# Three shared-expert tiles moved from behind the first router's picks into the last iterations of attention

## What is computed

```python
x = x + cross_attention(layernorm(x), ctx)        # 8 heads of 32, 77 keys
x = x + ffn0(layernorm(x))    # 8 experts of 704, top 2 of 8 by softmax, and a shared expert of 352:
                              # (silu(h @ Sg) * (h @ Su)) @ Sd for every row
x = x + patches(layernorm(x)) # a matmul with W_in and a lookup by a running count
x = x + ffn1(layernorm(x))    # 32 experts of 128, top 6 in groups, and a shared expert of 512
```

## Time and profile before

| | |
|---|---|
| median of 3 runs | 775.14 us (771.28 to 779.2) |
| the profiled execution | 776.99 us, of which its span 775.2 us |
| PE busy | 689.3 us, 89% of the span |
| DVE, ACT, POOL busy | 54%, 36%, 40% |
| granted TensorE clock | 0.947 of full speed on average |

### The profile page before, as it was taken

One profiled execution on the slowest core, in us unless ns is written; L12 is line 12 of the kernel. 1 busy time (PEld: TensorE's weight loads), 2 busy tenths in 40 slices (PEclk: granted clock), 3 DMA queues, 4 the chain that ended last, 5 costly groups with the idle time before them and its releaser, 6 DMA issues.

```text
span 775.2 us, 14150 instructions
## 1 busy us (share of the span) xinstructions
PE 689.3 (89%) x4526; PEld 611.6 (79%) x4526; DVE 415.7 (54%) x1613; ACT 276.4 (36%) x620; POOL 308.1 (40%) x322
## 2 busy tenths in 40 slices
PE   3868888999999999999999989889786999989836
PEld 2657677899999999999999979866554999978724
DVE  3998947423333343444684367457521666667823
ACT  2545743222111111133222322242321677767510
POOL 2323410770001010100035504554774477777770
PEclk9897966999999999999999999999989899999988
DMA  8999998236767676855587853363667777788976
GB/s 260 396 323 263 259 248 233 104 109 241 249 210 235 211 236 211 287 191 178 180 299 249 296 181 133 133 227 120 217 208 216 257 237 249 229 328 285 364 252 247
DMA packets 93535, 181.23 MB, mean 234 GB/s; under 512 B 9857, under 2 KB 54998, under 8 KB 93182
## 3 DMA queue, kind: packets, MB, share of 16 engines
q1 hardware_dynamic: 78048, 138.67, 57.5%
q0 software_dynamic: 13344, 38.68, 13.2%
q10 hardware_dynamic: 2046, 2.71, 1.1%
HBM read 134.07 MB, written 65.62 MB: 258 GB/s over the span
## 4 chain that ended last, share of the span: by engine, by line
PE 65%; DVE 13%; POOL 7%; DMA 6%; issue 5%; ACT 2%; DVEq 1%; SPq 0%; POOLq 0%; ACTq 0%
PE PB L596 22%; PE PB L634 14%; PE PB L610 6%; POOL rows_out L1891 4%; PE PB L803 3%; PE PB L794 3%; POOL rows_in L1852 3%; DMA X<-in_x 2%; PE PB L782 2%; PE PB L740 2%; PE PB L661 2%; DMA MEM<-rows_out 2%; PE PB L578 1%; DVE WK L1231 1%; DVE M L1240 1%
## 5 line engine op out<-in xcount | busy, mean ns | idle before, releaser
L596 PE MATMUL PB<-XT,MEM 128*128 128x128 f32 x1584 | 185.0, 276 | 0.3 <-issue 0.3
L596 PEld LDWEIGHTS PB<-XT,MEM 128*128 128x128 f32 x1584 | 180.7, 192 | 0.6 <-issue 0.5
L1843 POOL DMA_INDIRECT sorted_y<-WK x36 | 34.5, 959 | 244.2 <-DVE WK L1445 243.3
L1852 POOL DMA_INDIRECT rows_in<-MEM x96 | 93.9, 979 | 45.4 <-issue 28.5
L634 PE MATMUL PB<-MEM,WK 128*128 x432 | 101.3, 385 | 1.9 <-DVE MEM L1606 1.9
L634 PEld LDWEIGHTS PB<-MEM,WK 128*128 128x128 f32 x432 | 80.7, 193 | 12.1 <-issue 2.3
L917 ACT ACTIVATE XT<-PB 128x256 f32<-128x256 f32 x52 | 19.8, 381 | 146.2 <-PE PB L578 146.2
L1891 POOL DMA_INDIRECT rows_out<-WS,MEM x58 | 57.0, 983 | 32.7 <-issue 15.6
L803 PE MATMUL PB<-MEM,WK 128*128 x228 | 59.8, 386 | 8.3 <-DVE WK L1784 8.0
L1891 POOL DMA_INDIRECT rows_out<-MEM x56 | 54.7, 977 | 17.1 <-issue 15.5
L926 ACT ACTIVATE WK<-PB 128x640 f32<-128x640 f32 x36 | 25.3, 703 | 83.8 <-PE PB L596 83.8
(11 more groups left out here) (279 smaller groups left out, 1232.9 us busy)
## 6 DMA issues: line engine op xcount, KB each, us to landing
MEM<-in_w SPq DMA_DIRECT2D x36, 896.0 KB, 7.1
rows_in<-in_consts SPq DMA_DIRECT2D x32, 600.0 KB, 12.2
MEM<-in_w SPq DMA_DIRECT2D x36, 512.0 KB, 3.7
MEM<-rows_in SPq DMA_DIRECT2D x58, 300.0 KB, 3.9
MEM<-rows_out SPq DMA_DIRECT2D x16, 768.0 KB, 7.7
MEM<-in_w SPq DMA_DIRECT2D x32, 256.0 KB, 3.5
MEM<-in_w SPq DMA_DIRECT2D x2, 3072.0 KB, 19.0
sorted_x<-MEM SPq DMA_DIRECT2D x1, 5070.0 KB, 40.5
```

Source lines behind the costliest of these rows:

```text
L596: t = e.matmul(o[:, to:to + P], UPW[m][i % (3 - m)][:, k, c * P:(c + 1) * P], XT[:, n % 2, k, :], start=(k == 0), stop=(k == 1))
L1843: e.indirect_dma_start(out=DY, out_offset=bass.IndirectOffsetOnAxis(ap=DEST[:, i:i + 1], axis=0), in_=YS[:, i % 2, :], in_offset=None).the ...
L1852: e.indirect_dma_start(out=DX1, out_offset=bass.IndirectOffsetOnAxis(ap=SLOT1[:, i, j:j + 1], axis=0), in_=XR[:, i, :], in_offset=None).th ...
```

## The change

`FILL = 3`: shared tiles 0, 1 and 2 are taken out of the item loop, which now starts at n = 3, and their parts are written into the last iterations by hand, for PE, ACT and DVE. `EARLY` stays 14; SP and POOL are unchanged.

- **PE.** turn_x(0) at the end of iteration 17, turn_x(1) at the end of 18. The gate half of tile 0 at the head of 18, its up half behind values(15). The gate half of tile 1 at the end of 19; in 20 its up half between router(11) and the turns of tiles 12 and 13, and down(0) behind these. Behind the loop turn_x(2), down(1), the gate half of tile 2, then the counting matmuls, which now also wait for h(0), then tile 2's up half and turn_x(3).
- **Banks.** Tile 0 uses banks 5 and 2, the turned inputs the upper half of bank 7 and then bank 5. So the first half waits until the last probabilities are copied out ("pt", 15).
- **ACT.** The copies of turned inputs 0 and 1 at the end of 17 and 18; gates(0) in 19 and gates(1) in 21, each behind `turned_rows` and ahead of `router_rows`; the copy for tile 2 in 22; gates(2) behind the exponential.
- **DVE.** hidden(0) behind the statistics of iteration 19. hidden(1) between `max` and `max_index` of the first part of the picks, result(0) behind that `max_index`, result(1) behind "mm". hidden(2) and then the expert table behind "slot0". The three instructions for the shares stand at the end of the chain to "slot0" instead of ahead of the wait for the counts.

```diff
-EARLY = 14
+EARLY, FILL = 14, 3
...
-            return (0, 2) if n >= EARLY + nb else (3 * (n % 2), 3 * (n % 2) + 1)
+            return (5, 2) if n == 0 else (0, 2) if n >= EARLY + nb else (3 * (n % 2), 3 * (n % 2) + 1)
+
+        def turn_place(n):
+            return PB[:, 7, D:2 * D] if n < 2 else PB[:, 5, 0:D] if n < FILL else PB[:, 6, 0:D]
...
+            def shared_up(n, m, nb=NBLK):
+                q.wait_ge("xtb", n)
+                q.wait_ge("in_ws")
+                if n < FILL:
+                    q.wait_ge("s1", NT - 1)
+                    q.wait_ge("pt", NT - 1)
...
             for n in range(NT + 7):
                 if 0 <= n - 1 < NT:
                     scores(n - 1)
                 if n < NT:
                     queries(n, routed)
+                if n == NT + 2:
+                    shared_up(0, 0)
                 for i in ROUTED.get(n, ()):
                     router(i, n)
                 if 0 <= n - 3 < NT:
                     values(n - 3)
                 if 0 <= n - 2 < NT:
                     turn_probs(n - 2)
+                if n == NT + 2:
+                    shared_up(0, 1)
+                if n == NT + 4:
+                    shared_up(1, 1)
                 for i in ROWS.get(n - 1, ()):
                     router_turn(i, n)
                     routed[i % 2] = i
+                if n in (NT + 1, NT + 2):
+                    turn_x(n - NT - 1, NBLK)
+                if n == NT + 3:
+                    shared_up(1, 0)
+                if n == NT + 4:
+                    down(0, NBLK)
...
-            q.wait_ge("lgc", 1)
-            turn_x(0, NBLK)
+            turn_x(2, NBLK)
+            down(1, NBLK)
+            shared_up(2, 0)
+            q.wait_ge("h", 0)
             q.wait_ge("mm")
...
+            shared_up(2, 1)
+            turn_x(FILL, NBLK)
-            for n in range(SPLIT):
+            for n in range(FILL, SPLIT):
...
+                if n in (NT + 3, NT + 5):
+                    gates((n - NT - 3) // 2, NBLK)
+                if n == NT + 6:
+                    turned_x(2)
...
+            gates(2, NBLK)
+            turned_x(FILL)
...
                     if n > NT:
                         finish()
+                        hidden(0, NBLK)
...
                     t = e.max(m8[:, i, :], LG0[:, i, :])
                 t.then_inc(*q.mark("l0_v"))
-                q.wait_ge(*q.last)
+                t = q.last
+                if k == 0:
+                    hidden(1, NBLK)
+                q.wait_ge(*t)
                 for i in range(lo, hi):
                     t = e.max_index(i8[:, i, :], m8[:, i, :], LG0[:, i, :])
                 t.then_inc(*q.mark("l0_v"))
+                if k == 0:
+                    result(0, NBLK)
...
+            placed = q.last
+            q.wait_ge("pre")
+            e.tensor_scalar(PR[:, 0, :], PR[:, 1, :], 1.0, None, ALU.add).then_inc(*q.mark("l0_v"))
...
-            for n in range(SPLIT):
+            hidden(2, NBLK)
+            expert_table()
+            for n in range(FILL, SPLIT):
```

More of the change, by code:

```diff
@@ L541, in router @@
                 t.then_inc(*q.mark("lg", i))
[L543 to L559, removed]
             regs, busy = {}, {}
@@ L601, in up @@
                 else:
-                    q.wait_ge("xtb", n)
-                    q.wait_ge("in_ws")
                     q.wait_ge("h", n - 1 if n >= EARLY + nb else n - 2)
[L605 to L612, removed]
+                    for m in range(2):
+                        shared_up(n, m, nb)
                     between(n, nb)
@@ L895, in patches @@
                              ACT.Copy).then_inc(*q.mark("dpa", k))
[L897 to L912, removed]
             def turned_x(n):
                 q.wait_ge("tx", n)
+                q.wait_ge("scores", NT - 1)
                 q.wait_ge("up1", n - 2)
-                e.activation(XT[:, n % 2, :, :].rearrange("p c t -> p (c t)"), PB[:, 6, 0:D], ACT.Copy).then_inc(
+                e.activation(XT[:, n % 2, :, :].rearrange("p c t -> p (c t)"), turn_place(n), ACT.Copy).then_inc(
                     *q.mark("xtb", n))
@@ L1265, in dve_program @@
             e.tensor_copy(TRB[:], CC[:, CTR:CTR + P]).then_inc(*q.mark("trb"))
[L1267 to L1289, removed]
-                q.wait_ge(*q.last)
-                for i in range(lo, hi):
-                    t = e.max_index(i8[:, i, :], m8[:, i, :], LG0[:, i, :])
-                t.then_inc(*q.mark("l0_v"))
@@ L1459, in block_iteration @@
                     hidden(n, nb)
+            for n in range(NT + 7):
+                if 0 <= n - 1 < NT:
+                    scores(n - 1, n % 4 == 3 and n + 1 < NT or n % 4 == 1 and n > 8 or n == 16)
+                if 0 <= n - 4 < NT:
+                    stats(n - 4, "st", "o2", n - 4)
+                if 0 <= n - 3 < NT:
+                    values(n - 3)
+                for f, *k in jobs.get(n, ()):
+                    f(*k)
+                if n % 4 == 3 and 4 <= n < NT + 4:
+                    behind.append(norm_steps(n // 4 - 1, ("st", n - 4), False))
+                    if n > NT:
+                        finish()
+                        hidden(0, NBLK)
+                if n == NT + 4:
+                    logits(0, 0, NT - 4)
@@ new lines, in dve_program, with tiles @@
+            result(1, NBLK)
+            PRE = PB[:, 5, 0:128].rearrange("p (t e) -> p t e", t=NT)
+            upto, before = PAGE_U[:, 8:40].rearrange("p (g e) -> p g e", g=4), PAGE_U[:, 0:32].rearrange(
+                "p (g e) -> p g e", g=4)
+            ge = T1.rearrange("p (g t e) -> p g t e", g=4, t=4)
+            def tiles(v):
+                return v.unsqueeze(2).broadcast_to([P, 4, 4, 8])
+            for v in (PAGE_U[:, 0:8], PAGE_G[:, 0:1], PAGE_F[:, 0, :]):
+                t = e.memset(v, 0.0)
```

219 lines of the change are left out of this document (131 added, 88 removed).

## The result

The changed kernel takes 779.82 us (median of 20 executions, 774.83 to 785.8), the kernel before 776.33 (20 executions on the same chip, 769.5 to 781.31). The ratio is 1.0059, 95% interval 1.0036 to 1.0081: slower by 0.6%, 4.6 us by the ratio and 3.5 by the medians. The forecast was +5.6 us.

The account below looks back on a forecast made before the run. Two chains, PE's tiles and the scatter's weights 4.15 us ahead, bound block 0's start; block 0 +4.6 us from a late "slot0", plus 1.0 for clock, gives +5.6: 780.7 us median, range 771.7 to 787.5.

Parts of the forecast that it names:

- The head: Ahead of the counts: five up halves, two downs and two turns net added, 9.7 us at full clock, 19.4 at half.
- C: Rival: all added work fits in waits and "slot0" hardly moves; block 0 3.4 us earlier, 771.7 us; chance 0.05.
- Rival B: Clock in the head released at once, full from 109.65; "slot0" +3.6, block 0 -0.6 us, 774.5 us; chance 0.20.
- The 120 us of the forecast: PE's clock in the head: at half until 120 us, at full from there on.
- hidden(1) ahead of `max_index`: DVE at the picks: hidden(1) waits for gates(1) until 128.85, so `max_index` loses its cover, a wait of 3.39 us.
- R: End of the counts on PE: 127.4 before, forecast 135.5, with down(1), a half and counts of about 1.1 us.
- R to "slot0": Stretch behind the counts' end: 6.65 us as before, plus 0.7 for the three share instructions.
- "slot0" to block 0: Scatter chain: weights land 49.5 us behind "slot0" and start block 0, PE waiting some 4.5 us for them.
- The forecast's 1.0 for the clock: Block 0's first matmuls may run at half clock after PE's wait: nothing up to 3.4 us, taken as 1.0.
- The cap: At block 0: the gain from three fewer tiles is cut to 4.15 us less whatever "slot0" is late.
- E: Rival: PE alone decides when block 0 starts; three cycles, 12.5 us, saved, 762.6 us; chance 0.04.
- D: Rival: half clock up to the counts; block 0 +14.6 us, 789.7 us; chance 0.19 with all above +7.75.

Follow-up runs that it names:

- a_turn: Changed kernel with turn_x(14) put behind tile 13's up-projection on PE, its copy behind tile 13's silu on ACT: 893.51 us, ratio 1.0032 to the kernel before.
- b_plus4: Kernel before with four of POOL's 32 scatter sends done once more ahead of the others and waited for: 900.59 us, ratio 1.0116.
- a_dve: Changed kernel with DVE's first twelve max_index directly behind max, then result(0), then hidden(1): 893.03 us, ratio 0.9998 to the kernel before.
- a_all: Changed kernel with DVE's picks first, turn_x(14) behind tile 13's ups and the first three weight transfers early: 890.04 us, ratio 0.9988 to the kernel before.
- The delayed pair: Kernel before and changed kernel, both with sixteen chained memsets on POOL between "slot0" and the first send: 916.21 and 924.96 us.
- b_hole: Kernel before with only tile 0's gate half moved into PE's wait for "mm", ahead of the counts: 891.62 us, ratio 0.9980.
- a_again: Changed kernel, nothing edited, run on the slower kind of chip: 894.59 us against 891.69 for the kernel before, ratio 1.0031.
- b_delay: Kernel before with sixteen chained memsets on POOL between "slot0" and the first send: 916.21 us, ratio 1.0249 to the kernel before.

## Why the prediction was right

The sign and the main mechanism came out as forecast: "slot0" is late, the scatter's chain carries that to block 0, and the three removed tiles turn into a wait of PE. The time came out close, +4.6 us by the ratio where +5.6 was given, and that is in part luck, as the last point says. Step by step, against the profiled execution:

- *The head.* PE's first half at 109.16 after a wait of 1.31 for its copy (forecast 109.65), the norm of tile 15 done at 120.38 (120.8), the clock back at full at 120.0 (near 120), the last routers' end at 128.65 (128.7). Only the turns of tiles 12 and 13 were further off, at 123.94 (125.0). C fell with a "slot0" 10.8 late.
- *Rival B (release by 113)* fell in this execution, as the clock was at half until 120.0. But where the half clock ends is not a property of this kernel. In the other seven traces with the same head it ended between 110.0 and 120.8; windows of a_turn:

```profile
102.60:112.60 10.00, 8.70 (x42) 8.29 (x41) 1.85 (x6) 4.28 (x10) 0.98 (x2) 0.50 1.03 256
112.80:126.20 13.40, 12.76 (x103) 11.67 (x102) 5.90 (x39) 7.76 (x19) 1.03 (x2) 1.00 1.04 268
```

- *The 120 us of the forecast,* taken from the one trace of the kernel before, were thus near the late end of what occurs. B's sum did not come with its condition either: "slot0" of a_turn is 8.2 later than in b_plus4 on the same chip (141.52 - 133.35), where B had +3.6, for its way from the last routers to the counts is 7.63 all the same.
- *hidden(1) ahead of `max_index`.* Forecast as lost cover, and a_dve measures it: 2.9 us of the 5.1, with 0.9 of clock in them.
- *R, forecast 135.5, was 137.70.* The step "with the clock at half until 120 and full from there" failed in its second part. The clock fell again at 130.2, in the wait for result(0), and from the start of down(1) to the counts it took 5.25 instead of 2.6 us. The counts took 1.44 instead of 1.1, and down(1) started 0.7 earlier than forecast. The second fall wasn't chance: in all eight traces with the changed head the clock fell again between 123.7 and 131.0, also in a_dve and a_all, where PE had no wait over 0.3 us ahead of it.
- *R to "slot0".* 7.12 us, forecast 7.35, with the three share instructions in it. The table loads lay where the forecast put them.
- *"slot0" to block 0.* The forecast let the weights end it at + 49.5. The weights did come at + 49.7, but PE stood earlier, at turn_x(14), for the sorted rows, and the ups of tile 13 (5.33 us, at half clock) and down(12) (1.51) behind that wait ended last. Block 0 came at + 51.7. The step "after the change PE waits some 4.5 us for the weights" named the wrong transfer and left out the queue behind the other one. The forecast's 1.0 for the clock was put behind the start of block 0; there it was nothing, as the 44 instructions of block 0 took 5.08 in both kernels. The clock's part lay ahead of that start instead, and was some 2.1: with the weights 0.2 late, a miss of 1.2 us in sum.
- *The cap.* "The gain from the three tiles is cut to 4.15 us less whatever "slot0" is late" held: 10.8 late, 4.15 gained, 2.2 for queue and clock at block 0 make the 8.85. The delayed pair shows it with PE's own work out of the way. E (PE alone decides) thus fell where it was forecast for; on the chips with stops PE does decide and the late counts still eat the gain. D (half clock up to the counts) fell: it was half, full, half.
- *The size.* The profiled pair gave +8.8, above the +5.6 and inside the range that the forecast had left to D; the medians gave +3.5. The misses in that trace, 2.0 at "slot0" and 1.2 at block 0, both go the same way and make the 3.2 between +5.6 and +8.8. Over the 20 executions the time goes with the mean granted clock: 0.940 in the slowest, which is the profiled one, and 0.954 to 0.966 in the five fastest (774.83 to 777.32 us). So a usual execution has less half clock than the profiled one, and where it is less was not seen, as no such execution was profiled on this chip. If it is less in the head, as in most of the other traces, that makes up for what the forecast left out, and its number is near the measured one because two errors of opposite sign met. This part stays open.

The Trainium skill ("ScalarE: Activation LUTs", "What ACT_TABLE_LOAD costs") has a drain of some 1.4 us beside the load for a switch of sets, with which the sum would have been +7.0. The trace doesn't agree: ACT's timeline of the changed kernel has the copy ahead of the load, the load and the silu back to back.

```profile
121.04 0.38 ACT L909 ACTIVATE XTR<-PB 128x256 f32<-128x256 f32 x1 [0.51 <-PE PB L532]
121.44 1.28 ACT L944 ACT_TABLE_LOAD   x1
122.73 0.38 ACT L944 ACTIVATE WK<-PB 128x256 f32<-128x256 f32 x1
```

## What to carry to other kernels

Before moving work out of a stretch, find the second chain that ends beside it and how far it is behind: here it was 4.15 us, so three tiles (12.5 us) could bring no more than that, and their new place was at the head of that very chain. Of work put into an idle stretch, only what fits inside one engine's wait costs nothing, and b_hole shows that what it saves can vanish in the next wait; an instruction that waits for another engine (hidden(1) for silu) makes all that is queued behind it wait as well. And where a wait is forecast, look for the first instruction in the queue that needs the late chain, not the last. A clock read off one trace is one execution's: look at several before a forecast hangs on when it rises.

## What the runs showed of the hardware that was not expected

**The scatter stops other engines on some chips.** On four chips the kernel before took 891 to 893 us, against 776 on the first. Windows of a_again, in and behind the 32 sends (142.98 to 182.67):

```profile
158.00:175.00 17.00, 2.57 (x10) 1.75 (x10) 0.61 (x2) 0.00 (x0) 12.80 (x14) 0.60 0.28 102
175.00:190.00 15.00, 6.07 (x18) 4.56 (x19) 1.31 (x4) 1.20 (x4) 6.74 (x7) 0.50 0.33 102
190.00:219.20 29.20, 29.20 (x217) 27.75 (x216) 7.67 (x26) 6.12 (x20) 0.00 (x0) 0.96 0.27 92
```

PE is in the midst of its shared tiles, yet it is busy 2.57 of 17 us, and DVE and ACT 0.61 and 0.00. In PE's timeline the idle time ahead of such an instruction is put down to "issue", that is, to nothing that the profile shows:

```profile
165.95 0.37 PE L582 MATMUL PB<-XT,WS 128*96 128x128 f32 x1 [2.09 <-issue]
175.68 2.90 PE L631 MATMUL PB<-WS,WK 128*128 128x256 f32 x6 [9.36 <-issue]
```

The stops begin some 14 us behind the first send and end some 6 behind the last (the last one ends at 188.43). POOL's own step is unchanged, 1.27 us from send to send. On the first chip the same stretch has no such idle time: in the kernel before PE is busy all of the 29 us from 147 to 176. That the stops go with the sends, and not with PE's tiles, b_delay shows: with only memsets on POOL, PE is busy 45.59 of the 48 us from 135 to 183,

```profile
135.00:183.00 48.00, 45.59 (x350) 43.15 (x348) 15.75 (x39) 10.16 (x33) 47.20 (x15) 1.00 0.00 1
```

and delaying the scatter by 57.4 us made the kernel before only some 25 us longer (916.21 against 891.53), as PE by then has no work left to be stopped in. This is the smaller part of what these chips cost. The changed kernel's span is 111.8 us longer in a_again than on the first chip (895.8 against 784.0): 22.6 of it by block 0 and 89.2 behind it. There the first 261 us have no stops (PE busy 260.52 of 260.80), and the rest lies in what follows 480, which was not followed up. What in these chips makes the engines stop is open.

**The clock fell three times between 100 us and block 0, once before the change.** It fell at 102.9, 0.8 us behind the end of a wait of PE of 1.6, and at 130.2 and 188.3, in the midst of waits of 2.10 and 3.49; it was back at full at 120.0, 137.1 and 195.1. In the kernel before it also fell at 102.9 and was back at 130.2. That a wait brings the clock down is not shown: in a_dve it fell at 125.6 and in a_all at 123.7, with no wait of PE over 0.3 us in the 8 us before. What the half clock cost can be read off: 2.7 us on down(1) and the half of tile 2 (5.67 instead of 2.95), and 2.5 on the ups of tile 13 (5.33 instead of 2.82), of which 2.1 moved block 0.
